# Four graph networks in one program: the edge-row sends written out with fixed places in the list, and divided differently between two stages

## The reference

```
L0 (GIN, twice):  h = relu((x + segment_sum(x[src], dst)) @ W1 + b1) @ W2 + b2
L1 (attention with 4 heads, twice): softmax over the edges of a node
L2 (GCN + GRU gates, 4 blocks): segment_sum((h * norm)[src], dst) -> gates -> h
L3 (edge network): W   = silu(edge_attr_64 @ W1 + b1) @ W2 + b2
                   agg = zeros.at[src].add(x[dst] * W)
                   out = x + silu(agg @ W3 + b3) @ W4 + b4
```

## Time and profile before

| | |
|---|---|
| median of three runs | 6173.88 us |
| profiled execution, its own time | 6172.0 us |
| span from first to last instruction | 6170.3 us |
| busy: PE, DVE, POOL, ACT | 4048.0, 3623.8, 3525.0, 1133.2 us |
| sends (L1869), count, busy | 168 / 173.2 us in counting; 150 / 146.4 in g0; 32 / 37.1 in edge tables; 432 / 424.5 in the GRU blocks |

### The profile page before, as it was taken

One profiled execution on the slowest core, in us unless ns is written; L12 is line 12 of the kernel. 1 busy time (PEld: TensorE's weight loads), 2 busy tenths in 40 slices (PEclk: granted clock), 3 DMA queues, 4 the chain that ended last, 5 costly groups with the idle time before them and its releaser, 6 DMA issues. The chain is left out here.

```text
span 6170.3 us, 100975 instructions
## 1 busy us (share of the span) xinstructions
PE 4048.0 (66%) x25279; PEld 2952.6 (48%) x25280; DVE 3623.8 (59%) x8665; ACT 1133.2 (18%) x2056; POOL 3525.0 (57%) x3627
## 2 busy tenths in 40 slices
PE   3444456591477777774366666665778778888874
PEld 1111124461266565653356555653555556656653
DVE  7555541345699999997466666665211245555553
ACT  0222220103111111111211111112211222222221
POOL 0232326204577777771477777762666667777771
PEclk7555568795689999997577767778889888888886
DMA  4000032101344444442322222224212222222223
GB/s 202 24 18 15 17 138 94 45 13 55 108 120 124 120 123 121 118 125 73 125 83 80 76 81 82 82 62 163 63 56 62 72 73 79 78 78 79 78 78 40
DMA packets 332132, 512.58 MB, mean 83 GB/s; under 512 B 103981, under 2 KB 245337, under 8 KB 322130
## 3 DMA queue, kind: packets, MB, share of 16 engines
q0 software_dynamic: 129376, 287.12, 17.1%
q1 hardware_dynamic: 202610, 223.92, 11.1%
HBM read 407.89 MB, written 102.87 MB: 83 GB/s over the span
## 5 line engine op out<-in xcount | busy, mean ns | idle before, releaser
L1174 POOL DMA_INDIRECT e_ring<-att_rows,e_near x1760 | 1786.9, 1015 | 554.4 <-issue 476.5
L1243 PE MATMUL e_psum<-e_ring,e_whole_pick 128*128 128x264 f32 (+1 forms) x3520 | 850.5, 395 | 231.6 <-DVE e_ring L1408 224.7
L1952 POOL DMA_INDIRECT e_nodes<-x,e_edges x832 | 801.4, 963 | 267.6 <-issue 241.4
L1243 PEld LDWEIGHTS e_psum<-e_ring,e_whole_pick 128*128 128x128 f32 x3520 | 652.5, 230 | 356.8 <-issue 154.2
L1198 PE MATMUL e_px<-t_parts,e_pick 128*128 x5280 | 675.7, 269 | 98.7 <-DVE e_pick L1306 51.5
L1322 DVE TENSOR_TENSOR e_prod<-e_px,e_ring 128x512 f32<-128x512 f32 x660 | 450.1, 682 | 404.8 <-DMA e_ring<-att_rows,e_near 284.6
L403 PE MATMUL b_acc<-b_pick_key,b_pick_lo 128*128 128x400 bf16 x984 | 337.2, 515 | 382.8 <-issue 363.1
L1869 POOL DMA_INDIRECT sorted<-rx_held,rx_index x432 | 424.5, 983 | 218.7 <-issue 209.0
L1198 PEld LDWEIGHTS e_px<-t_parts,e_pick 128*128 128x128 bf16 x5280 | 445.8, 108 | 185.8 <-issue 116.4
L1286 ACT ACTIVATE e_whole_pick<-e_pturn 128x512 f32<-128x512 bf16 x440 | 261.9, 595 | 1358.1 <-PE e_pturn L1234 1340.3
L1312 DVE TENSOR_REDUCE e_dots<-e_prod 128x8 f32<-128x512 f32 (+1 forms) x660 | 445.0, 674 | 0.0
(11 more groups left out here) (374 smaller groups left out, 6520.0 us busy)
## 6 DMA issues: line engine op xcount, KB each, us to landing
e_relb<-place SPq DMA_DIRECT2D x56, 1024.0 KB
e_ring<-att_rows,e_near POOLq DMA_INDIRECT x1760
sorted<-o_fill SPq DMA_DIRECT2D x11, 2508.0 KB
e_edges<-sorted SPq DMA_DIRECT2D x209, 132.0 KB
kept<-gin_counts SPq DMA_DIRECT2D x5, 4000.0 KB
rx_held<-in_edge_rows POOLq DMA_DIRECT2D x52, 297.0 KB
e_nodes<-x,e_edges POOLq DMA_INDIRECT x832
gru_late<-kept SPq DMA_DIRECT2D x3, 4000.0 KB, 32.4
```

The costliest lines, as they stand in the source:

```text
L1174: pool.indirect_dma_start(out=ring[:, s, r, 0:wd + HEADS], out_offset=None, in_=xrows, in_offset=bass.IndirectOffsetOnAxis(ap=near[:, s, r ...
L1243: mm = pe.matmul(psum[q % 2][:, 0:RING], whole_pick[:, q % 2, c, :], ring[:, s, q * G + c, :], start=(c == 0), stop=(c == G - 1))
L1952: pool.indirect_dma_start(out=nodes[:, q, u, :], out_offset=None, in_=source, in_offset=bass.IndirectOffsetOnAxis(ap=edges[:, q, u, RBF + ...
```

## The change

All senders lose their hardware loops: the batches are written out by a Python loop, so that every address is a constant. The sends read their places from the list itself (`slot[:, at:at+1]`); the copy into `index`, the drain and the two `index` tiles are gone, and so is the load past the last batch with its wait. The loop in `build_counts` around the sends and `add_own` is written out as well. The division is changed: counting takes 10 sends per batch (240 in all), g0 takes 6 batches of 13 (78); edge tables (32) and GRU blocks (108 each) keep theirs.

```diff
 def add_own(t):
     pool.wait_ge(moved, t * PER + PER)
-    block_ = flat[:, ds(t * (NP + P), P)]
+    block_ = flat[:, t * (NP + P):t * (NP + P) + P]
     pool.tensor_tensor(block_, block_, K["identb"][:, :], ALU.add).then_inc(diag, 1)
-sender.send(pool, 0, 0, first=True)
-add_own(0)
-with pool.Fori(0, NT // 2 - 1) as j:
-    sender.send(pool, j, 1)
-    add_own(j * 2 + 1)
-    sender.send(pool, j + 1, 0)
-    add_own(j * 2 + 2)
-sender.send(pool, NT // 2 - 1, 1)
-add_own(NT - 2)
-add_own(NT - 1)
+for t in range(NT):
+    if t < NT - 1:
+        sender.send(pool, t)
+    add_own(t)
...
-COUNT_SENDS = (0, 7, NT - 1)
-GIN_SENDS = (7 * (NT - 1), 15, 10)
+COUNT_SENDS = (0, 10, NT - 1)
+GIN_SENDS = (10 * (NT - 1), 13, 6)
...
 class Sender:
-        self.index = [m.sb(f"{tag}x_index{s}", [P, size], I32) for s in range(2)]
...
-    def send(self, pool, j, s, first=False):
-        n, full = j * 2 + s, self.size * 16
-        pool.wait_ge(self.loaded[s], j * 16 + 16)
-        pool.tensor_copy(self.index[s][:, :], self.slot[:, ds(n * self.size, self.size)])
-        pool.drain()
+    def send(self, pool, n):
+        pool.wait_ge(self.loaded[n % 2], n // 2 * 16 + 16)
         for u in range(self.size):
-            if u == self.size // 2:
-                if not first:
-                    pool.wait_ge(self.sent[1 - s], j * full + s * full)
-                self.load(pool, n + 1, 1 - s)
-            pool.indirect_dma_start(out=self.D["sorted"], in_=self.held[s][:, u, :], in_offset=None,
-                                    out_offset=bass.IndirectOffsetOnAxis(ap=self.index[s][:, u:u + 1], axis=0)
-                                    ).then_inc(self.sent[s], 16)
+            if u == self.size // 2 and n + 1 < self.batches:
+                if n:
+                    pool.wait_ge(self.sent[1 - n % 2], (n + 1) // 2 * self.size * 16)
+                self.load(pool, n + 1)
+            at = n * self.size + u
+            pool.indirect_dma_start(out=self.D["sorted"], in_=self.held[n % 2][:, u, :], in_offset=None,
+                                    out_offset=bass.IndirectOffsetOnAxis(ap=self.slot[:, at:at + 1], axis=0)
+                                    ).then_inc(self.sent[n % 2], 16)
     def run(self, pool):
         self.begin(pool)
-        self.send(pool, 0, 0, first=True)
-        with pool.Fori(0, self.batches // 2 - 1) as j:
-            self.send(pool, j, 1)
-            self.send(pool, j + 1, 0)
-        self.send(pool, self.batches // 2 - 1, 1)
+        for n in range(self.batches):
+            self.send(pool, n)
         self.end(pool)
     def end(self, pool):
...
-        pool.wait_ge(self.loaded[n % 2], n // 2 * 16 + 16)
```

More of the change, by code:

```diff
@@ L724, in _ @@
                 sender.begin(pool)
-                sender.send(pool, 0, 0, first=True)
-                sender.send(pool, 0, 1)
+                sender.send(pool, 0)
+                sender.send(pool, 1)
                 sender.end(pool)
@@ L1705 @@
 ROWW = RBF + 2
-COUNT_SENDS = (0, 7, NT - 1)
-GIN_SENDS = (7 * (NT - 1), 15, 10)
-TABLE_SENDS = (7 * (NT - 1) + 150, 16, 2)
-GRU_SENDS = [(7 * (NT - 1) + 182 + 108 * b, 9, 12) for b in range(4)]
-NSC = 7 * (NT - 1) + 182 + 432
+COUNT_SENDS = (0, 10, NT - 1)
+GIN_SENDS = (10 * (NT - 1), 13, 6)
+TABLE_SENDS = (10 * (NT - 1) + 78, 16, 2)
+GRU_SENDS = [(10 * (NT - 1) + 110 + 108 * b, 9, 12) for b in range(4)]
+NSC = 10 * (NT - 1) + 110 + 432
 SROWS = (NGRP + 1) * EGRP
@@ L1847, in __init__, with load @@
         self.sent = [m.sem(f"{tag}x_sent{s}") for s in range(2)]
-    def load(self, pool, n, s):
-        pool.dma_start(self.held[s][:, :, :], self.D["edge_rows"][:, ds(n * self.size + self.first, self.size), :]
-                       ).then_inc(self.loaded[s], 16)
+    def load(self, pool, n):
+        first = self.first + n * self.size
+        pool.dma_start(self.held[n % 2][:, :, :], self.D["edge_rows"][:, first:first + self.size, :]
+                       ).then_inc(self.loaded[n % 2], 16)
@@ L1853, in begin @@
     def begin(self, pool):
-        pool.dma_start(self.slot[:, :], self.D["slot"][:, ds(self.first, self.batches * self.size)]).then_inc(self.listed, 16)
-        self.load(pool, 0, 0)
+        pool.dma_start(self.slot[:, :], self.D["slot"][:, self.first:self.first + self.batches * self.size]).then_inc(self.listed, 16)
+        self.load(pool, 0)
         pool.wait_ge(self.listed, 16)
-    def send(self, pool, j, s, first=False):
-        n, full = j * 2 + s, self.size * 16
-        pool.wait_ge(self.loaded[s], j * 16 + 16)
-        pool.tensor_copy(self.index[s][:, :], self.slot[:, ds(n * self.size, self.size)])
-        pool.drain()
-        for u in range(self.size):
-            if u == self.size // 2:
-                if not first:
-                    pool.wait_ge(self.sent[1 - s], j * full + s * full)
-                self.load(pool, n + 1, 1 - s)
-            pool.indirect_dma_start(out=self.D["sorted"], in_=self.held[s][:, u, :], in_offset=None,
-                                    out_offset=bass.IndirectOffsetOnAxis(ap=self.index[s][:, u:u + 1], axis=0)
-                                    ).then_inc(self.sent[s], 16)
+    def send(self, pool, n):
+        pool.wait_ge(self.loaded[n % 2], n // 2 * 16 + 16)
+        for u in range(self.size):
+            if u == self.size // 2 and n + 1 < self.batches:
[6 more added lines that the diff above has]
+                                    ).then_inc(self.sent[n % 2], 16)
@@ L1873, in run @@
     def run(self, pool):
         self.begin(pool)
-        self.send(pool, 0, 0, first=True)
-        with pool.Fori(0, self.batches // 2 - 1) as j:
-            self.send(pool, j, 1)
-            self.send(pool, j + 1, 0)
-        self.send(pool, self.batches // 2 - 1, 1)
+        for n in range(self.batches):
+            self.send(pool, n)
         self.end(pool)
     def end(self, pool):
-        n, full = self.batches, self.size * 16
         for s in range(2):
-            pool.wait_ge(self.sent[s], (n + 1 - s) // 2 * full)
@@ L1886, in end @@
-        pool.wait_ge(self.loaded[n % 2], n // 2 * 16 + 16)
+            pool.wait_ge(self.sent[s], (self.batches + 1 - s) // 2 * self.size * 16)
 def edge_messages(nc, K, D, source, agg):
```

## The result

The changed kernel takes 6076.74 us (median of 4 runs, 6072.0 to 6079.73), the kernel before 6172.8 beside it (4 runs, 6170.4 to 6177.79). The ratio on record is 0.9838, 95% interval 0.9826 to 0.985; the two medians by themselves give 0.9844. The prediction was 6071 with a range of 6058 to 6092. The profiled spans are 6170.3 and 6076.0 us.

The account below looks back on a forecast made before the run. POOL's 150 sends bound g0 for its last 87 us, PE and DVE before that; POOL alone worked at a GRU block's end. 6172.0 - 87.0 - 15.7 = 6069.3, plus 1.9 for the median: 6071 us, range 6058 to 6092.

Parts of the forecast that it names:

- g0, 87.0 us: g0: with 78 sends for 150, POOL ends before PE and DVE, so the closing barrier's wait goes, saving 87.0 us.
- GRU blocks, 15.7 us: Four GRU blocks: without copies and drains POOL no longer holds the closing barrier, saving its excess of 15.7 us.
- Rival C: GRU blocks: something other than POOL holds their barrier, so only g0 gains; 6087 us, chance 0.06.
- Counting, 0: Counting stage: 72 sends more fit into POOL's idle time, costing 0; bounds 96 us lost to 10 us gained.
- sum of 102.7 us: Whole kernel: the total predicted gain, 87.0 us from g0 and 15.7 us from the GRU blocks.
- 18.8 us stall: g0's second batch before the change: 18.80 us gap before its first send, while stores of the counts fill the DMA engines.
- rival B: g0: the stall comes from straight code beside stores, at every batch, 5 x 18.8 = 94 us; 6118 us, chance 0.07.
- Rival D: Counting: added sends hold up the stage one for one, by the shared port, 96 us; 6167 us, chance 0.05.
- Rival E: POOL's sends in GRU blocks and g0: each pays for straight code to arrive; at 0.5 us each, 6227 us, chance 0.05.
- PE's clock in g1, at most 2 us: Start of g1: PE's pause before it is 87 us shorter and might bring a higher clock; at most 2 us, none counted.
- The rest, 0: Outside g0, GRU blocks and counting: edge tables' written-out sends and dropped loads were counted as 0.

Follow-up runs that it names:

- new-division run: The kernel before with only the new division of sends, still in loops with a copy and drain per batch: 6088.56 us, ratio 0.986.
- drain-per-batch run: The changed kernel with one POOL drain at each batch start of all senders, without copies and loops: 6083.75 us, ratio 0.9852.
- drain per tile: The changed kernel plus one POOL drain per counting tile, before `add_own`: 6069.99 us; again, beside the changed kernel's 6075.78, 6068.32 us (both ratios 0.9826).
- written out with the old division: The changed kernel with the kernel before's division (7 sends per counting tile, 10 batches of 15 in g0): 6141.66 us, ratio 0.9946.

## Why the prediction was right, and where it missed

- **g0, 87.0 us.** Right: 86.6, with the barrier row at 0.4 over both stages. POOL's last send was to end at 994 to 1016; the stage started 5.9 us later than before, so that is 1000 to 1022, and it ended at 1015.74. Batch 1 began at 914.16, which is 0.8 us ahead of my 909 to 931 when those are moved by the same 5.9. That its middle would wait for batch 0 to land was in the text; that batch 2's load would then be late by 9.06 us was not, nor that POOL's closing drain would take 7.00 us for the 1.37 of before. It ends at 1024.2, and SP comes to the barrier at 1050.0: the cover made both free, not the working. The new-division run shows that the division earned it.
- **GRU blocks, 15.7 us.** Right: 16.5. The batch takes 11.97 us for the 11.99 worked out. POOL ends 154.5 us after the blocks' start, where I had 155.5 (4417.5 less 4262.0). Rival C (another engine holds this barrier) fell with the row's 0.7 us, and more sharply in the drain-per-batch run: there only POOL was slowed, and the row came back to 15.3.
- **Counting, 0.** The step that missed; its real size is +4.9 us. "So `add_own` is as early as before, and nothing is queued behind it but the next batch": the first half was right (0.2 us earlier), the second was wrong for the last tile, behind which the barrier's own drain is queued. I counted the drains in the batches as removed and never asked what the one that remains would then do. The same term was missing in g0 and in the GRU blocks, where the closing drain grew from 1.37 to 7.00 and from 0.88 to 2.02 us; there other engines end later and hide it. With the drain per tile the stage takes 715.6, 0.7 less than before, and the sum of 102.7 us is nearly whole: that span is 6068.5 against 6170.3, 101.8 less. Part of this is luck, since 2.4 us of g1 that the sum did not have stand against 5.4 lost in the rest.
- **The 18.8 us stall and rival B.** B (the stall belongs to straight code and comes at every batch) fell: the steady batches of g0 start at gaps of 0.30. I left its cause open; it was the drain, waiting for sends in flight.
- **Rival D, the sends hold up counting.** It fell: pairs of PE groups take 11.55 and 11.58 us, DVE's picks last 258 and 326 ns on average where they lasted 255 and 324, and the sends last 1004 ns where they lasted 1031:

```profile
L1861 POOL DMA_INDIRECT sorted<-bx_held,bx_slot x240 | 241.0, 1004 | 74.6 <-issue 69.4 <-DMA bx_held<-in_edge_rows 5.1
L1861 POOL DMA_INDIRECT sorted<-g0x_held,g0x_slot x78 | 75.7, 971 | 49.9 <-DMA g0x_held<-in_edge_rows 27.0 <-issue 22.9
```

- **Rival E, straight code is slower.** It fell: of the 108 written-out sends of the first GRU block those behind the first batch keep a step of 1.26 us, 0.30 of it between them. The sends of the first batch are longer, up to 1.67 us, but up to 1.56 in the loop kernel too. The Trainium skill (Runtime: NRT & Kernel Launch, section "Instruction fetch mechanics") says that the fetch of straight code runs ahead of execution and is mostly hidden; the trace agrees, with this step of 1.26 us.
- **PE's clock in g1, at most 2 us.** 2.4 came, but at its start the clock rose no earlier than before. Two later dips are gone. The stretch from 40 to 70 us behind the barrier ran at a granted clock of 0.94 before, and at 1.00 after (1.00 is the upper of its two levels, 2.4 GHz, and 0.50 the lower), with nine matmuls more recorded; the 5 us from 110 us on ran at 0.66 before and at 1.00 after. DVE's work falls behind that of the changed kernel by 0.5 us at the first dip and by 1.6 at the second. The first, before:

```profile
1170.90:1200.90 30.00, 27.06 (x175) 19.42 (x173) 17.22 (x31) 4.56 (x7) 0.00 (x0) 0.94 0.04 12
```

and after:

```profile
1090.20:1120.20 30.00, 27.08 (x184) 19.47 (x183) 17.22 (x31) 4.55 (x7) 0.00 (x0) 1.00 0.04 13
```

g1 took 274.3 to 274.6 us in the two kernels in which PE had idled for 63 us or more before it, and 272.0 to 272.4 in the other three of the table and in the run with a drain per tile. No run set out to test that link, and the dips do not stand at one place: written out with the old division, g1 has neither of these two, and falls behind by 1.6 us in its last 15 us, at granted clocks of 0.84 and 0.82.
- **The rest, 0.** It took 6.3 us more (1.8 to 6.3 in the nine other traces), 0.3 of it in the edge tables and the others spread over stages whose code is the same. Of these, 1.4 stand in a stage that ends before the first send. There is one trace of the kernel before, so how much belongs to that execution is not known. Not explained.

Between the spans the forecast missed by 8.4 us (102.7 less 94.3): the closing drain 4.9, this rest 6.3 and g0 0.4, less 2.4 from g1 and 0.8 from the GRU blocks. Between the medians it missed by 5.7 only, since the profiled execution before stood 1.9 us below its median, and that of the changed kernel (6077.9 us) 1.2 above: luck, and not the working.

## What to carry to other kernels

Removing a drain from a loop need not remove all that it paid for: look at the next instruction of the same kind, above all at the stage's closing barrier, and ask whether the bill falls due there. A drain that must be paid belongs where its engine idles anyway; here one more instruction per tile gained 7.5 us, 5.6 of them at one closing barrier, in a kernel from which 84 drains had been removed. And where a stage is bound by one engine's list, move the list first and polish its steps second: moving 72 sends into idle time gave 87 us, taking copies, loops and drains out of the GRU batches 16.5, of which 13.7 are the drains.

## What the runs showed of the hardware

- A drain on POOL costs 81.4 ns per DMA that POOL has issued since its last drain, and some 65 ns, though all of them have landed. The line was read between 13 and 109 DMAs; closing drains of the other kernels lie on it (8: 0.71 us, 11: 0.96, 16: 1.37, 35: 2.92, 85: 7.00). Somewhere between 109 and 121 the cost falls by some 97 DMAs' worth; from 121 to 193 it is 90 to 102 short of the line, at 265 it is 195 short.
- A drain on POOL also waits for sends in flight: it lasted 18.26 us in the stretch in which the DMA engines are full, while POOL had nothing else to do but a copy of 0.20, and ended 0.7 us after the last landing. At a batch start of a GRU block the drain in the drain-per-batch run ended 0.45 us after the last landing and 1.68 after POOL's last send.
- The Trainium skill (VectorE: DVE Perf Modes, section "The DRAIN you can't avoid") tells of a flush behind each DVE operation and of a drain that opens and closes a program, some 12 ns and constant on all engines. POOL's drains here are not constant: those of the closing barriers took 34 ns where it had done nothing in the stage, and 0.7 to 7.5 us behind the sends.
